# A masked-attention layer on one Trainium2 core: bias sums on VectorE, scales from squares, value weights ahead of the last quarter of a product, and turned tiles two parts ahead

## What is computed

```python
def reference(x, adj, W_q, b_q, W_k, b_k, W_v, b_v):   # x 4096 x 512, adj 4096 x 4096 of 0 and 1
    h = jnp.maximum(_layernorm(x), 0.0)
    q = h @ W_q.T + b_q
    k = h @ W_k.T + b_k
    v = h @ W_v.T + b_v
    z = (q @ k.T) / math.sqrt(512) * adj
    z = jnp.where(z == 0.0, -10000.0, z)
    return x + jax.nn.relu(jax.nn.softmax(z, axis=1) @ v)
```

## Time and profile before

| | |
|---|---|
| median of three runs | 1463.7 us (1463.51 to 1463.74) |
| the profiled execution's own time | 1463.89 us |
| its span, first to last instruction | 1462.1 us |
| PE busy | 1449.8 us, 99% |
| DVE busy | 1301.7 us, 89% |
| ACT busy | 868.2 us, 59% |
| granted TensorE clock | 1.00 throughout |

### The profile page before, as it was taken

The page is one execution under the profiler, slowest core; times in us unless marked ns, Lnnn a source line. Parts: engine busy times, 40 slices in busy tenths (PEclk is TensorE's granted clock), DMA queues, the critical chain, the costliest instruction groups (busy, mean ns, idle before and its releaser), DMA issues.

```text
span 1462.1 us, 24721 instructions
## 1 busy us (share of the span) xinstructions
PE 1449.8 (99%) x9414; PEld 924.2 (63%) x9414; DVE 1301.7 (89%) x1597; ACT 868.2 (59%) x1398; POOL 44.8 (3%) x27
## 2 busy tenths in 40 slices
PE   8999999999999999999999999999999999999999
PEld 4455556766666666666666666666666666666555
DVE  7979888898999899998989898989898999987986
ACT  4666666765656566655665565656566566655542
POOL 0000000000000000100010001000000001000100
PEclk9999999999999999999999999999999999999999
DMA  6587666375555665566556664666456655664252
GB/s 209 162 270 215 219 182 244 137 297 187 223 216 226 215 241 216 220 218 243 204 202 248 224 233 186 225 245 239 188 225 245 234 187 203 245 216 178 90 162 97
DMA packets 100533, 307.53 MB, mean 210 GB/s; under 512 B 33856, under 2 KB 34112, under 8 KB 98624
## 3 DMA queue, kind: packets, MB, share of 16 engines
q1 hardware_dynamic: 100416, 305.96, 58.5%
...
## 4 chain that ended last, share of the span: by engine, by line
PE 93%; DVE 4%; ACT 1%; issue 1%; DMA 0%; SPq 0%; POOL 0%; DVEq 0%; ACTq 0%
PE o L688 45%; PE za L630 22%; PE zd L630 11%; PE zb L630 5%; PE o L617 4%; PE o L597 4%; PE zb L688 1%; DVE stats L1117 1%; PE za L699 0%; DVE g_buf L1197 0%; DMA slots<-in_L_gnn_W_q 0%; ACT g_buf L839 0%; DVE slots L1291 0%; DVE slots L1169 0%; DVE slots L1287 0%
## 5 line engine op out<-in xcount | busy, mean ns | idle before, releaser
L688 PE MATMUL o<-v_buf,p_buf 128*128 128x512 f16 x3072 | 726.4, 376 | 0.8 <-DVE p_buf L1323 0.6
L688 PEld LDWEIGHTS o<-v_buf,p_buf 128*128 128x128 f16 x3072 | 300.5, 98 | 260.9 <-issue 1.5
L630 PE MATMUL za<-h_buf,g_buf 128*128 128x256 f16 x2952 | 402.2, 273 | 1.6 <-ACT um_tmp L888 0.7
L630 PEld LDWEIGHTS za<-h_buf,g_buf 128*128 128x128 f16 x2952 | 287.3, 98 | 140.0 <-DVE g_buf L1197 3.7
L630 PE MATMUL zd<-h_buf,g_buf 128*128 128x256 f16 x1476 | 201.3, 273 | 0.0
L908 ACT ACTIVATE slots<-slots,log_p 128x1024 f32<-128x1024 f32 x128 | 146.0, 1141 | 51.5 <-DVE slots L1316 51.4
L1323 DVE TENSOR_TENSOR p_buf<-slots,p_buf 128x1024 f16<-128x1024 f32 x128 | 157.4, 1230 | 14.5 <-PE zb L688 13.6
L1316 DVE TENSOR_TENSOR slots<-slots,floor_b 128x1024 f32<-128x1024 f32 x128 | 170.0, 1330 | 0.3 <-POOL floor_b L547 0.3
L1279 DVE TENSOR_TENSOR slots<-um_tmp,dm_tmp 128x512 f32<-128x512 f32 x128 | 89.2, 697 | 78.7 <-ACT dm_tmp L893 78.7
L903 ACT ACTIVATE slots<-za,c_all,kappa 128x256 f32<-128x256 f32 x128 | 72.2, 564 | 142.4 <-PE za L630 141.5
L1291 DVE SCALAR_TENSOR_TENSOR slots<-slots 128x1024 f32<-128x1024 f32 x128 | 156.0, 1219 | 0.2
...
## 6 DMA issues: line engine op xcount, KB each, us to landing
g_buf<-g_dram SPq DMA_DIRECT2D x108, 896.0 KB, 5.5
v_buf<-v_dram SPq DMA_DIRECT2D x128, 512.0 KB, 3.4
...
g_dram<-g_buf SPq DMA_DIRECT2D x12, 896.0 KB, 5.5
...
h_buf<-h_dram SPq DMA_DIRECT2D x7, 1024.0 KB, 8.8
```

Source lines behind the costliest of these rows:

```text
L630: mm = pe.matmul(bank[:, 0:QH], g_of(i)[:, a, op, j, :], right[b][j], start=(fresh and j == 0 and m == 0), stop=(j == 1 and m == 2), skip_ ...
L688: mm = pe.matmul(bank, a[:, kt, span], v_buf[:, n % V_BUFS, kt, b, c:d], start=(j == 0 and kt == 0 and m == 0), stop=(j == PAIRS - 1 and k ...
```

## The change

It rebuilds the first 45 us and re-times the turned tiles.

- w and u: instead of four float32 matmuls each with a bias column as weights, ACT and DVE add up W_k and W_q, row by row scaled by the bias (`add_w`, `add_u`), and PE sums over the partitions with a matrix of ones: one matmul of 512 columns for w, four of one column for u. The biases arrive laid out as they are needed.
- Scales: from the root of the sum of squares instead of the largest value. ACT squares W_v in one instruction of 2048 elements per row and M in four; PE sums W_v's over the partitions, POOL M's.
- M is computed by rows of the weights as they arrive (e), into four banks at once. W_v is loaded ahead of the last quarter of W_k and W_q, and the last quarter of M is spread between transposes.
- v of tiles 0 to 3 is projected in a stretch of its own before the loop, which now begins with part 4. h tiles are ready two tiles ahead of their v, not four. Of the row buffers two remain, and g of quad 0 uses one bank.
- In the loop, `row_tile(k)` = k + 2 replaces k + 4. The statistics of quad g + 2 move from the parts with i = 1 to those with i = 3; `quad_rstd` (now for quad g + 1) and `key_terms` move from i = 3 to i = 1. On SP, the transposes and the load of x move behind other issues.

```diff
+        def row_tile(k):
+
+            return k + 2 if k + 2 < TILES else -1
...
         def gT_bank(q, i):
-            return o_bank[1] if i % 2 == 1 else o_bank[3]
+            return o_bank[1] if q > 0 and i % 2 == 1 else o_bank[3]
...
             load_wk(0)
+            sp.dma_start(b_cols[:, 0, :], bq).then_inc(bq_loaded, 16)
+            load_wq(0)
+            sp.dma_start(b_cols[:, 1, :], bk).then_inc(bk_loaded, 16)
             load_first_x(0)
             load_wk(1)
-            sp.dma_start(b_cols[:, 1, :], bk.rearrange("(k p) -> p k", p=P),
-                         allow_slow_non_contiguous=True).then_inc(bk_loaded, 16)
+            load_wq(1)
             load_first_x(1)
             load_wk(2)
-            load_wk(3)
+            load_wq(2)
             load_first_x(2)
             load_first_x(3)
-            for e in range(KC):
-                sp.dma_start(wq_raw[:, e, :], wq[e * P:(e + 1) * P, :]).then_inc(wq_loaded[e], 16)
             sp.dma_start(wv_raw, wv_t.rearrange("(k p) n -> p k n", p=P)).then_inc(wv_loaded, 16)
+            load_wk(3)
+            load_wq(3)
             load_x(1)
...
-                if 1 <= g < QUADS:
-                    store_h(g)
                 if g == QUADS - 1:
                     load_h(1)
                 if 1 <= g < QUADS:
@@ -476,21 +491,24 @@
                 if g >= 2:
                     store_g(2 * (g - 2))
                     store_g(2 * (g - 2) + 1)
+                if 2 <= g < QUADS:
+                    turn_h(QUAD * g + 2)
+                if 1 <= g and g + 2 < QUADS:
+                    load_x(g + 2)
                 if 2 <= 2 * g - 3 < PAIRS:
                     load_adj(2 * g - 3)
-                if 1 <= g < QUADS - 1:
-                    turn_h(QUAD * g + QUAD)
-                    turn_h(QUAD * g + QUAD + 1)
+                if 2 <= g < QUADS:
+                    turn_h(QUAD * g + 3)
                 if g < QUADS:
                     store_v(2 * g)
                 if 1 <= g < QUADS - 1:
-                    turn_h(QUAD * g + QUAD + 2)
-                if g + 3 < QUADS:
-                    load_x(g + 3)
-                if 1 <= g < QUADS - 1:
-                    turn_h(QUAD * g + QUAD + 3)
+                    turn_h(QUAD * g + QUAD)
+                if 1 <= g < QUADS:
+                    store_h(g)
                 if 2 <= 2 * g - 2 < PAIRS:
                     load_adj(2 * g - 2)
+                if 1 <= g < QUADS - 1:
+                    turn_h(QUAD * g + QUAD + 1)
...
-                elif q == 0 and i == 1:
+                elif q == 0 or q == 1 and i == 0:
+                    pe.wait_ge(g_copied, KC * q + i)
+                else:
                     pe.wait_ge(h_lo_ready, TURNED)
-                else:
                     pe.wait_ge(g_copied, KC * q + i - 1)
...
-            def product_m(d):
-                for e in range(KC):
-                    if d == 0:
-                        pe.wait_ge(wq_loaded[e], 16)
+            def products_m(e, first, last):
+
+                pe.wait_ge(wk_loaded[e], 16)
+                pe.wait_ge(wq_loaded[e], 16)
+                for d in range(first, last + 1):
                     mm = pe.matmul(m_bank[d][:, :], wk_raw[:, e, d * P:(d + 1) * P], wq_raw[:, e, :],
                                    start=(e == 0), stop=(e == KC - 1))
...
-            pe.wait_ge(wide_ready, KC)
-            for e in range(KC):
-                pe.wait_ge(wk_loaded[e], 16)
-                mm = pe.matmul(w_bank[:, :], bq_wide[:, e, :], wk_raw[:, e, :], start=(e == 0), stop=(e == KC - 1))
-            mm.then_inc(w_ready, 1)
-            product_m(0)
+            products_m(0, 0, 3)
+            products_m(1, 0, 3)
+            products_m(2, 0, 3)
+            pe.wait_ge(ones_ready, 1)
+            pe.wait_ge(square_v_ready, 1)
+            pe.matmul(norm_bank, ones[:, :], square[0][:, 0:1], start=True, stop=True).then_inc(square_v_summed, 1)
+            pe.wait_ge(w_part_ready, KC)
+            pe.matmul(w_bank[:, :], ones[:, :], w_part, start=True, stop=True).then_inc(w_ready, 1)
+            products_m(3, 0, 0)
             pe.wait_ge(ident_ready, 1)
             transpose_h(0)
+            products_m(3, 1, 2)
             transpose_h(1)
-            pe.wait_ge(bk_loaded, 16)
-            for e in range(KC):
-                mm = pe.matmul(u_row_bank, b_cols[:, 1, e:e + 1], wq_raw[:, e, :],
-                               start=(e == 0), stop=(e == KC - 1))
-            mm.then_inc(u_row_ready, 1)
-            transpose_h(2)
-            transpose_h(3)
-            product_m(1)
-            pe.wait_ge(u_row_copied, 1)
+            products_m(3, 3, 3)
+            pe.wait_ge(u_part_ready, KC)
             for d in range(KC):
-                mm = pe.transpose(u_bank[:, d:d + 1], u_row[:, d * P:(d + 1) * P], ident[0:1, 0:1])
+                mm = pe.matmul(u_bank[:, d:d + 1], u_part[:, d * P:(d + 1) * P], ones[:, 0:1], start=True, stop=True)
             mm.then_inc(u_ready, 1)
-            product_m(2)
-            product_m(3)
-
-            for k in range(PARTS):
+            for t in range(QUAD):
+                project_v(t)
+                transpose_h(t + 2)
+
+            for k in range(QUAD, PARTS):
                 g, i = k // QUAD, k % QUAD
                 begun, ended = opening_pair(k), opening_pair(k - 1)
...
+            def square_m(k):
+                act.wait_ge(m_ready, k + 1)
+                nc.scalar.activation(m_square[:, k, :], m_bank[k][:, :], ACT.Square,
+                                     accum_out=square[1][:, k:k + 1]).then_inc(square_m_ready, 1)
...
             square_root(0)
+            act.wait_ge(wv_loaded, 16)
+            nc.scalar.activation(wv_square, wv_raw.rearrange("p k n -> p (k n)"), ACT.Square,
+                                 accum_out=square[0][:, 0:1]).then_inc(square_v_ready, 1)
+            normalise(0)
+            act.wait_ge(square_v_summed, 1)
+            nc.scalar.activation(top[0][:, :], norm_bank, ACT.Sqrt).then_inc(norm_ready, 1)
+            normalise(1)
+            high_wv(0)
+            high_h(0)
+            high_wv(1)
             act.wait_ge(w_ready, 1)
             nc.scalar.copy(w_all, w_bank[:, :]).then_inc(w_copied, 1)
-            normalise(0)
...
-                if g + 1 < QUADS:
-                    high_h(k + QUAD)
+                if row_tile(k) >= 0:
+                    high_h(row_tile(k))
                 if k in (5, 6):
                     high_t(0, 2 * (k - 5))
                     high_t(0, 2 * (k - 5) + 1)
-                if k + QUAD + 1 < TILES:
-                    normalise(k + QUAD + 1)
-                if k == 2:
+                if row_tile(k + 1) >= 0:
+                    normalise(row_tile(k + 1))
+                if k == QUAD:
                     square_root(2)
-                    for d in range(KC):
-                        high_m(d)
                 if not between and 1 <= g <= QUADS:
                     copy_g(g - 1, i)
-                if i == 2 and 1 <= g and g + 2 < QUADS:
-                    square_root(g + 2)
+                if i == 0 and 2 <= g < QUADS - 1:
+                    square_root(g + 1)
...
+            def add_w(e):
+                dve.wait_ge(wk_loaded[e], 16)
+                dve.wait_ge(w_part_ready, e)
+                v.scalar_tensor_tensor(out=w_part, in0=wk_raw[:, e, :], scalar=b_cols[:, 0, e:e + 1], in1=w_part,
+                                       op0=ALU.mult, op1=ALU.add).then_inc(w_part_ready, 1)
+
+            def add_u(e):
+                dve.wait_ge(wq_loaded[e], 16)
+                dve.wait_ge(u_part_ready, e)
+                v.scalar_tensor_tensor(out=u_part, in0=wq_raw[:, e, :], scalar=b_cols[:, 1, e:e + 1], in1=u_part,
+                                       op0=ALU.mult, op1=ALU.add).then_inc(u_part_ready, 1)
+
...
+            low_h(4)
+            dve.wait_ge(squares_reduced, 1)
+            v.tensor_reduce(square_sum[:, :], square_all[:, :], AX_X, ALU.add).then_inc(square_sum_ready, 1)
+            low_v(2)
+            magnitude(1)
+            v.tensor_scalar(kappa[:, :], up_inv[1][:, :], SCALE / UNIT, None, ALU.mult).then_inc(kappa_ready, 1)
+            link(v.tensor_scalar(u_cols[:, :], u_cols[:, :], up[1][:, 0:1], None, ALU.mult))
+            row_dot(4)
+            low_m(0)
+            low_m(1)
+            low_m(2)
+            low_m(3)
+            low_h(5)
+            low_v(3)
+            row_dot(5)
+
...
-                if i == 3 and 1 <= g and g + 2 < QUADS:
-                    quad_rstd(g + 2)
-                if k < QUAD:
-                    low_v(k)
-                if k == 3:
-                    low_m(2)
-                    low_m(3)
-                    quad_rstd(2)
+                if i == 1 and g + 1 < QUADS:
+                    quad_rstd(g + 1)
...
-                if g + 1 < QUADS:
-                    low_h(k + QUAD)
+                if row_tile(k) >= 0:
+                    low_h(row_tile(k))
...
+                if k == QUAD:
```

(87 more changed lines are left out.)

143 lines of the change are left out of this document (69 added, 74 removed).

## The result

| | before | after |
|---|---|---|
| median of 10 runs | 1463.71 us (1463.51 to 1464.06) | 1467.78 us (1466.81 to 1468.18) |
| ratio to before, 95% interval | | 1.0027 (1.0018 to 1.0037) |
| profiled execution: time, span | 1463.89, 1462.1 | 1467.56, 1465.8 |
| v of tile 0 | 31.48 | 23.86 |
| part 9 (first scores) | 73.11 | 68.44 |

The changed kernel is 4.1 us slower, 0.27%. My range (1459.5 to 1468.5) holds it, but the likeliest case, no change within 0.2%, does not. The page after, as the earlier trace rows: span, busy time, chain.

The account below looks back on a forecast made before the run. PE was taken as the bound (busy 1449.8 of 1462.1 us), with DVE bounding parts 4 to 8. 1463.9 - 5.1 + 4.7 + 1.0 = 1464.5; likeliest 1464.3, own range 1461.5 to 1466.5, 8-in-10 range 1459.5 to 1468.5.

Parts of the forecast that it names:

- the likeliest case: Whole kernel: no change beyond 0.2% (2.9 us), as summed, at 1464.3 us; chance 0.48.
- Part one: The start, up to v of tile 0: v at 22.9 against 31.48, 8.6 us earlier.
- Part two: From 22.9 to part 9: DVE bounds parts 4 to 8, part 9 at 68.0 not 73.11, 5.1 us left.
- Part three: Parts 11-13, 15-17, 19-21, 23-25: statistics ahead of the urgent half make each 16.5 us; +4.7, bounds +3.5 to +6.
- Part four: Transposes of tiles 4g + 2 behind two stores of g make v wait: +1.0, bounds 0 and 7.5.
- What costs nothing: Parts 28 and 29: two more `low_h` cost nothing, as no v waits; likewise the longer lead lost for `copy_c12`.
- Rival 2: Turned tiles: `turn_h(4g + 2)` behind two stores lands late, five waits of 1.4 us, 1470 us, slower; chance 0.26.
- the sum of the forecast: Whole kernel: 1463.9 - 5.1 + 4.7 + 1.0 = 1464.5 us, against the median 1464.3.

Follow-up runs that it names:

- The kernel with the third burst behind: Changed kernel with the statistics of quad 3 moved from the end of part 7 to the end of part 8, behind low_g(0, 1): 1464.18 us.
- moved into the gaps: Changed kernel with the statistics of quads 4 to 7 moved into two gaps of DVE in the same part, around low_v: 1462.14 us, ratio to before 0.9988.
- with PE kept busy: Changed kernel with four products of zeros on PE ahead of the scores of part 9: 1466.35 us.

## Why the prediction came out as it did

1. **Part one, v of tile 0 at 22.9: nearly.** It came at 23.86, and by the path that the forecast had: v came 0.1 us behind the end of DVE's copy of u (PE's row names no releaser), and the copy stood right behind the last `low_wv`. The miss began with the load: W_v was there at 14.2 (forecast 13.3; late bound 15.1), its square took 1.91 (2.0), the root came at 16.85 (16.2) and `low_wv(3)` ended near 23.6 (22.7). The four u products of one column took 0.95 us, not 0.4 (eight records, 0.12 us each), but that was hidden: PE still stood 0.97 before v.
2. **Part two, part 9 at 68.0, DVE the bound: right.** DVE reached part 4 at 41.72 instead of 40.9, and from there it was 26.7 us instead of 27.1; 68.44, so -4.67 instead of -5.1. The kernel with the third burst behind shows the bound: take 2.9 us from DVE's list and part 9 comes 2.3 us sooner.
3. **Part three, 16.5 for each of four stretches, +4.7: right, by mechanism and size.** 16.54 or 16.55 four times, +4.76; moved into the gaps, 15.1 to 15.5.
4. **Part four, +1.0: too much by 0.8.** +0.23, at one tile. The value that I took lay between bounds, and the truth was near the lower one.
5. **"What costs nothing: the two `low_h` more in parts 28 and 29": wrong, +1.76.** I gave as the reason that no v waits for them. True, but `combine_t`, `combine_g` and `add_c2` stand behind them on DVE, which from 232.8 to 255 us rests only 0.20, and ACT's copy of the next pair waits for `add_c2`. I named who waits for the moved step's result, and not who is queued behind it. Of the 1.76, moving three `combine_t` gives back 1.1 in its trace, and shortening the two dots that moved with the `low_h` 0.5. No run took out the `low_h` themselves.
6. **The step that was missing: what the clock makes of a wait.** I forecast a wait of about 2.5 us at part 9, and counted it as 2.5. It cost up to 4.0, since the clock fell behind it: +1.60 in this trace, 1.4 by the medians with PE kept busy. This is also why PE's busy time fell by 3.4 and not by 5 to 6: the slowed products count as busy.

From forecast to measurement, in the spans: the sum of the forecast was +0.6; adding 0.43 (parts one and two), 0.06 (part three), -0.77 (part four), 1.76 and 1.60 gives +3.68. Rival 2 (1470, slower) gave the right sign for a cause that cost 0.23 here: without points 5 and 6 the profiled execution would have been at about 1464.2, no change. That the sign came out on the slower side is due to two steps that no case of mine contained. And the range held the result because rival 2 had stretched it up to 1468.5; that was luck.
